# Top-k attention: the copy of a pair's added results moves behind the next pair's first exponent pass on ScalarE

## What is computed

```python
q = heads(_conv1x1(x, Wq, bq)); k = heads(_conv1x1(x, Wk, bk)); v = heads(_conv1x1(x, Wv, bv))   # 8 heads of 32
scores = jnp.einsum('bhnd,bhmd->bhnm', q, k) * DHEAD ** (-0.5)
kth = jax.lax.top_k(scores, TOPK)[0][..., -1:]                                                    # TOPK = 64
masked = jnp.where(scores >= kth, scores, jnp.finfo(scores.dtype).min)
attn = jax.nn.softmax(masked, axis=-1)
o = jnp.einsum('bhnm,bhmd->bhnd', attn, v)
o = _conv1x1(o, Wo, bo) + x
h1 = jax.nn.relu(_batchnorm(_conv1x1(o, W1, b1), g1, be1)); h2 = _batchnorm(_conv1x1(h1, W2, b2), g2, be2)
return h2 + o
```

## Time and profile before

| | |
|---|---|
| median of three runs | 5078.21 us (5076.14 to 5078.52) |
| profiled execution | 5075.16 us, its span 5073.4 us |
| busy over the span | VectorE 85%, ScalarE 82%, TensorE 81%, GpSimd 30% |
| granted TensorE clock | mean 0.837 of full speed |

### The profile page before, as it was taken

The page is one execution under the profiler, slowest core; times in us unless marked ns, Lnnn a source line. Parts: engine busy times, 40 slices in busy tenths (PEclk is TensorE's granted clock), DMA queues, the critical chain, the costliest instruction groups (busy, mean ns, idle before and its releaser), DMA issues. The chain is left out here.

```text
span 5073.4 us, 107203 instructions
## 1 busy us (share of the span) xinstructions
PE 4120.5 (81%) x32161; PEld 2777.1 (55%) x32161; DVE 4332.4 (85%) x25624; ACT 4161.6 (82%) x6082; POOL 1502.7 (30%) x362
## 2 busy tenths in 40 slices
PE   8576677777777676777777777898999999999999
PEld 4344445544555444454554445444567777777776
DVE  3999999999999999999999999431378888888886
ACT  2799799999999799999999899544268888888885
POOL 0344445444455444444444444100100000000000
PEclk9777777777777777777777777899899999999999
DMA  6000000000000000000000000200420101111112
GB/s 217 7 18 17 7 17 17 9 17 16 9 18 17 7 17 8 18 18 8 18 18 17 9 17 11 64 6 0 157 73 25 34 25 34 27 32 34 25 34 95
DMA packets 79598, 154.63 MB, mean 30 GB/s; under 512 B 8120, under 2 KB 49464, under 8 KB 73528
## 3 DMA queue, kind: packets, MB, share of 16 engines
q1 hardware_dynamic: 78904, 146.72, 10.1%
HBM read 99.50 MB, written 47.19 MB: 29 GB/s over the span
## 5 line engine op out<-in xcount | busy, mean ns | idle before, releaser
L542 POOL TENSOR_TENSOR a_probs<-a_scores,a_probs 128x2304 f32<-128x2304 f32 x288 | 1460.6, 5092 | 1623.8 <-ACT a_probs L465 1623.8
L560 DVE MAX8 a_top<-a_scores 128x8 f32<-128x36 f32 x18432 | 1832.5, 182 | 31.9 <-ACT a_scores L449 23.4
L376 PE MATMUL a_ps_t<-ident,a_probs 128*128 128x128 f32 x5184 | 964.0, 322 | 521.1 <-ACT a_probs_t L460 378.5
L376 PEld LDWEIGHTS a_ps_t<-ident,a_probs 128*128 128x128 f32 x5184 | 666.7, 163 | 815.0 <-ACT a_probs_t L460 519.6
L1300 DVE TENSOR_SCALAR_CACHE_REDUCE b_soft<-b_ps_s 128x2304 f32<-128x2304 f32 x288 | 735.2, 2553 | 26.2 <-PE b_ps_s L1159 8.5
L465 ACT ACTIVATE a_probs<-a_scores,a_steep_kth 128x2304 f32<-128x2304 f32 x290 | 641.3, 2212 | 136.2 <-DVE a_minus_max L700 136.1
L460 ACT ACTIVATE a_probs_t<-a_ps_t 128x512 f32<-128x512 f32 (+1 forms) x1440 | 728.9, 548 | 14.8 <-PE a_ps_t L376 3.2
L1175 PE MATMUL b_ps_t<-ident,b_soft 128*128 128x128 f32 x5184 | 727.0, 276 | 1.6 <-DVE b_soft_t L1306 0.6
L1175 PEld LDWEIGHTS b_ps_t<-ident,b_soft 128*128 128x128 f32 x5184 | 577.2, 140 | 170.1 <-ACT b_soft_t L1264 60.1
L453 ACT ACTIVATE a_probs<-a_probs,a_minus_max 128x2304 f32<-128x2304 f32 x288 | 638.1, 2216 | 31.8 <-issue 18.1
L366 PE MATMUL a_ps_s<-a_k_stack,a_q_ring 128*128 128x512 f32 (+1 forms) x1465 | 650.8, 604 | 16.1 <-ACT a_scores L449 10.7
(11 more groups left out here) (133 smaller groups left out, 4135.9 us busy)
## 6 DMA issues: line engine op xcount, KB each, us to landing
a_k_stack<-k_parts SPq DMA_DIRECT2D x72, 288.0 KB, 6.0
b_k_stack<-k_parts SPq DMA_DIRECT2D x72, 288.0 KB, 6.0
a_q_ring<-q_parts SPq DMA_DIRECT2D x294, 64.0 KB
b_q_ring<-q_parts SPq DMA_DIRECT2D x294, 64.0 KB
k_parts<-p_high SPq DMA_DIRECT2D x36, 256.0 KB, 2.0
k_parts<-p_rest SPq DMA_DIRECT2D x36, 256.0 KB, 2.1
q_parts<-p_high SPq DMA_DIRECT2D x36, 256.0 KB, 2.0
q_parts<-p_rest SPq DMA_DIRECT2D x36, 256.0 KB, 2.0
```

What stands on the lines that cost most here:

```text
L376: last = pe.transpose(ps_t[(NTG * s + g) % 2][:, P * m:P * m + P], probs[s % 2][:, P * (m0 + m):P * (m0 + m) + P], cst["ident"][:, :])
L542: pool.tensor_tensor(probs[u][:, :], scores_all[:, 2 * (p % 2) + u, :], probs[u][:, :], ALU.subtract).then_inc(masked_ready, 1)
L560: last = dve.max(top8[s // 2 % 2][:, s % 2, c, :], scores_all[:, s % 4, CHUNK * c:CHUNK * c + CHUNK])
```

## The change

`exponentials` for a pair's first tile goes from the head of `pair_step` to its end, where it handles the first tile of the next pair (`s + 2`, of the next head if need be: `ahead`), and stands ahead of `finish`. The very first one is issued before the loop. The loop over heads runs seven times, and the eighth head is written out, without an exponent pass behind the last pair.

```diff
             def exponentials(s, h, tile, parity):
+                ahead, s = divmod(s, HEAD_TILES)
                 act.wait_ge(masked_ready, tile + 1)
                 act.activation(probs[s % 2][:, :], probs[s % 2][:, :], ACT.Exp, scale=SCALE,
-                               bias=minus_max[parity][:, s % 2:s % 2 + 1], accum_out=sums[:, s, cols(h, 1)]
+                               bias=minus_max[parity][:, s % 2:s % 2 + 1], accum_out=sums[:, s, cols(h + ahead, 1)]
                                ).then_inc(probs_ready, 1)
...
-            with act.Fori(0, HEADS) as h:
+            exponentials(0, 0, 0, 0)
+
+            def pair_step(p, h, last=False):
+                pair, tile, s, parity = h * HEAD_PAIRS + p, h * HEAD_TILES + 2 * p, 2 * p, p % 2
+                keep_scores(s + 4, tile + 4)
...
+                act.activation(parts[:, :], ps_o[:, 0:PAIR], ACT.Copy).then_inc(parts_ready, 1)
+                guess_place(0, pair + 2, parity)
+                if not last:
+                    exponentials(s + 2, h, tile + 2, 1 - parity)
+                finish(s, h, pair)
+
+            with act.Fori(0, HEADS - 1) as h:
                 for p in range(HEAD_PAIRS):
-                    pair, tile, s, parity = h * HEAD_PAIRS + p, h * HEAD_TILES + 2 * p, 2 * p, p % 2
-                    exponentials(s, h, tile, parity)
-                    keep_scores(s + 4, tile + 4)
...
-                    guess_place(0, pair + 2, parity)
-                    finish(s, h, pair)
+                    pair_step(p, h)
+            for p in range(HEAD_PAIRS):
+                pair_step(p, HEADS - 1, last=p == HEAD_PAIRS - 1)
```

More of the change, by code:

```diff
@@ L501, in _ @@
             guess_place(0, 1, 1)
-            with act.Fori(0, HEADS) as h:
-                for p in range(HEAD_PAIRS):
-                    pair, tile, s, parity = h * HEAD_PAIRS + p, h * HEAD_TILES + 2 * p, 2 * p, p % 2
-                    exponentials(s, h, tile, parity)
-                    keep_scores(s + 4, tile + 4)
[L507 to L525, removed]
-                    guess_place(0, pair + 2, parity)
-                    finish(s, h, pair)
@@ new lines, in _ @@
+            exponentials(0, 0, 0, 0)
+            def pair_step(p, h, last=False):
+                pair, tile, s, parity = h * HEAD_PAIRS + p, h * HEAD_TILES + 2 * p, 2 * p, p % 2
+                keep_scores(s + 4, tile + 4)
+                guess_place(1, pair + 1, 1 - parity)
+                keep_turned(s, 0, tile)
+                keep_turned(s, 1, tile)
+                exponentials(s + 1, h, tile + 1, parity)
+                keep_turned(s, 2, tile)
+                keep_turned(s, 3, tile)
+                keep_turned(s, 4, tile)
+                keep_scores(s + 5, tile + 5)
+                keep_any(pair + 1)
+                keep_turned(s + 1, 0, tile + 1)
+                keep_turned(s + 1, 1, tile + 1)
+                act.wait_ge(kth_ready, pair + 2)
+                penalty(0, 1 - parity)
+                keep_turned(s + 1, 2, tile + 1)
+                keep_turned(s + 1, 3, tile + 1)
+                keep_turned(s + 1, 4, tile + 1)
+                penalty(1, 1 - parity)
+                act.wait_ge(weighed, tile + MCH + 3)
+                act.activation(parts[:, :], ps_o[:, 0:PAIR], ACT.Copy).then_inc(parts_ready, 1)
[3 more added lines that the diff above has]
+                finish(s, h, pair)
```

## The result

| | before | after |
|---|---|---|
| median of 22 runs | 5077.35 us (5074.33 to 5079.53) | 5085.35 us (5083.03 to 5088.93) |
| ratio after to before | | 1.0016, 95% interval 1.0009 to 1.0022 |
| span of the profiled execution | 5073.4 us | 5082.5 us |
| granted TensorE clock | 0.837 | 0.845 |

What follows compares the result with a forecast made beforehand. A cycle through GpSimd, ScalarE and VectorE sets 20.54 us a pair, with GpSimd releasing the exponent pass. 13.2 + 0.6 - 3.7 - 2.6 - 1.2 = +6.3 us gives a median of 5084.5 us, range 5070 to 5097.

Steps and rivals of the forecast that it cites:

- GpSimd releases the exponent pass, not `finish`: Plain pairs: exponent pass starts 0.13 us behind GpSimd's subtraction in 125 of 143; moving `finish` leaves that start, gain 0.
- The rival of the recovered wait: Plain pairs: `finish` as releaser would give 0.25 us each, 31 us, with branches 39: 5039; chance 4%.
- Theory B: Whole change: the moved wait did pay, but something else in the new order took it back; no size or chance given.
- The slot: Between exponent pass and score copy: moved `finish` costs 0.12 us in 110 plain pairs of heads 1 to 7, +13.2 us.
- The rival of a hidden slot: Most pairs: VectorE or code placement absorbs the 0.12 us, leaving only the stalls' gain: 5071, or 5064; chance 13%.
- the dearer slot: Behind the exponent pass: `finish`'s PSUM read or code fetch makes it 0.22 us a pair: 5096; chance 11%.
- The written-out head: Last head, 15 plain pairs: constant waits return 0.08 us of the 0.12 slot, leaving 0.04 each, +0.6 us.
- The six back edges: Heads' ends: exponent pass covers ScalarE's branch, VectorE's becomes the limit; 0.3 to 0.9 us kept each, together -3.7 us.
- The rival of an unhidden branch: Heads' ends: branch taken only once `finish` leaves the queue; edges lose 0.3 us each, exit gives nothing: 5094; chance 12%.
- The exit: End of ScalarE's loop: seventh stall becomes a fall-through, -2.6 us; bound 0 if fetching new code stalls as long.
- What follows each stall: Pairs after each back edge: ScalarE no longer late, 0.2 us on each of six heads, -1.2 us; bounds 0 and 0.3.
- the 9 pairs that `finish` had held: Pairs after a long VectorE search, 11 in the prediction: exponent pass wins 0.1 us, pays 0.12; counted as 0.

Runs made afterwards that it cites:

- e2: Changed kernel with `finish` put back ahead of the exponent pass, loop of seven and written-out head kept: 5073.15 us, ratio to before 0.9986.
- e3m: Kernel before, with a second, idle copy of the sums into a spare tile directly ahead of `finish`'s own: 5079.03 us, ratio to before 1.0001.
- e4m: Changed kernel, with a second, idle copy of the sums directly ahead of `finish`'s own, behind the exponent pass: 5113.48 us, ratio to before 1.0069.
- e9: e7 with `finish` ahead of the exponent pass in every pair, ScalarE's and VectorE's head loops written out: 5054.62 us, ratio to before 0.9952.
- e10: e9 with `finish` behind the exponent pass, the changed kernel's order: 5066.24 us, ratio to before 0.9976.
- e1: Kernel before, order inside a pair kept, only ScalarE's loop run seven times and the eighth head written out: 5073.48 us, ratio to before 0.9989.
- e7: e6 with VectorE's seven loop rounds over heads written out too: 5053.92 us, ratio to before 0.9957.
- e6: e5 with all eight heads of ScalarE written out, VectorE's loop kept: 5060.88 us, ratio to before 0.9966.
- e8: Changed kernel with VectorE's back edge moved six pairs on, its loop over pairs 8 to 25: 5090.52 us, ratio to before 1.0026.
- e5: Changed kernel with `finish` of pairs 0 to 16 behind the next pair's count of doubts, pair 17's ahead of the exponent pass: 5074.43 us, ratio 0.9995.

## Why the prediction held, step by step

**GpSimd releases the exponent pass, not `finish`.** Right. The pass is 0.13 behind GpSimd in before, after and e2. Doubling the copy ahead of it costs nothing (e3m), doubling it behind costs its full slot in nearly every pair (e4m). The rival of the recovered wait, 5039, falls, and Theory B with it: e2 puts the wait back and is some 15 us faster than the changed kernel, and e9 against e10 shows the same without loops, 11.6 us.

**The slot.** Right in kind, mis-sized: 0.12 forecast, 0.104 measured (exponent start to score copy 2.318 instead of 2.215). The 98 plain pairs still came to +11.9 where 11.8 was forecast, and that is luck. At places 8 and 17 of a head, 13 of the 98, the step grew by only 0.02: VectorE starts one instruction of its selection (L594, now L603) 13.30 behind the threshold before and after the change, and also in e9 and e10, whatever ScalarE does, and what holds it there no run separates. So the slot cost 85 x 0.104 + 13 x 0.02 = 9.1 us. Four long pairs added 1.7 and small rises of the others 1.1. The rival of a hidden slot holds at those two places and falls everywhere else; the dearer slot of 0.22 falls too. The figure that the prediction took from the Trainium skill, page "ScalarE: Activation LUTs", gives 0.15 a step; the runs show 0.10, and the measurement decides.

**The written-out head.** The constant wait gave back 0.096 in each pair (0.034 behind GpSimd), where 0.08 was forecast, and the slot was 0.104: 0.0 instead of +0.6. The last head of e1 and all heads of e6, e9 and e10 show the same start, 0.03 behind GpSimd.

**The six back edges.** Right. ScalarE's branch is covered by the exponent pass except for 0.46, VectorE's branch is the next limit, and 0.73 an edge is kept on average (0.77 to 0.98 in five, 0.17 in one), where the forecast had 0.62 (3.7 over six). e7 shows that both branches are what lies above 20.44 there; e6 and e8 show that it is VectorE's that limits once ScalarE's is covered. The rival of an unhidden branch falls.

**The exit.** Right: -2.6. The fall-through into new code didn't stall (e1 -2.8, e2 -2.7), so the bound of 0 below falls.

**What follows each stall.** This step failed. It put 0.2 us a head to the gain. The seven pairs behind a head's first came to +0.4 where the slot alone is 7 x 0.104 = 0.7, so it gave 0.3 in all and not 1.2.

**What the sum hadn't.** Place 10 of a head: the exponent pass is 0.41 behind GpSimd instead of 0.13 in each of the seven loop heads, five of them plain pairs, +1.4 beyond the slot. The row of GpSimd, ending at 366.65, and of ScalarE there:

```profile
361.58 5.07 POOL L551 TENSOR_TENSOR a_probs<-a_scores,a_probs 128x2304 f32<-128x2304 f32 x1 [10.51 <-ACT a_probs L466]
```

```profile
367.06 2.21 ACT L454 ACTIVATE a_probs<-a_probs,a_minus_max 128x2304 f32<-128x2304 f32 x1 [0.91 <-POOL a_probs L551]
```

And the 9 pairs that `finish` had held cost 1.5 instead of 0. The step itself was right: the exponent pass wins 0.1, the slot costs 0.1, and the score copy starts when it did. But two of the nine stand at place 10 and lose 0.28 there, and three, one of these two among them, take late transposes of the kind shown with e4m (+0.47, +0.28, +0.25). These misses, up and down, leave +8.9 against +6.3 in the stage, and the medians 8.0 apart: that the forecast of 5084.5 came within 1 us owes something to them cancelling.

**Open.** The loss at place 10 is the same in all rounds of a kernel, so it hangs on the place in the code and not on the data. It is 0.28 in the changed kernel, e5 and e8, 0.14 in e2, and absent in before, e1, e4m and in the kernels with ScalarE written out. Those with VectorE written out lose at other places, 6, 11 and 16. That a fetch of code lies behind either is only argued. What brings TensorE's low clock onto the transposes that ScalarE takes next isn't settled either: pairs with transposes late by 0.25 us or more, edges aside, number 0 before, 3 in e1, 5 in e2, 9 after, 7 in e5 and 27 in e4m, without a rule that I could test. These two together are why e5 missed its forecast.

The best kernels measured are e7 and e9, which beat both: 0.43% and 0.48% under before. Their gain isn't the exponent pass's place but the branches (14.4 us at the edges, 3.1 at the exit) and the constant waits (0.10 in most pairs), less what VectorE loses at its own places.

## What to carry to other kernels

A wait in the profile is worth only what lies between it and the next thing that would have held the engine: look for the second releaser (here GpSimd, 0.13 us ahead of the exponent pass in 125 of 143 pairs) before moving work past it. In this kernel a short instruction was free in a hole and cost its whole slot, in nearly every iteration, where the next engine was waiting; two orders of the same two instructions were 12 to 15 us apart. What paid here, and is worth trying elsewhere: a long instruction ahead of a loop's branch to cover it, the engines' branches in the same iteration, and, where code size allows, the loop written out.

## What the hardware showed that I had not expected

- A wait on a constant lets the ACTIVATE start 0.03 us behind the releaser, a wait on a register's value 0.13 us: in a cycle of 20.5 us this is 0.5% for each such hand-over on it (e6, whose plain pairs have 20.46 against 20.55 in e5).
- 64 columns copied from PSUM directly behind an accumulator read take 0.10 us from start to next start, though their record says 0.20; the same copy ahead of an exponent pass takes 0.12.
- A few instructions at fixed places of a long loop body start 0.14 or 0.28 us late in every round (place 10 in e2, and in the changed kernel, e5 and e8), and an edit elsewhere moves or removes that (e1, e4m and e6 have none there). The cause is open.
- With TensorE at 1.2 GHz and busy without a hole, transposes reach ScalarE late by 0.2 to 0.6 us, and since ScalarE is on the cycle this ends as 0.4 to 1.0 us a pair, although over the whole pair TensorE is busy 16 of 21 us. Only pairs in which the low clock fell on those transposes (0.50 to 0.54 over that stretch) were long in this way.
